# The two-part split of the softmax maxima moves from VectorE to GpSimd in a fused four-layer kernel

## What is computed

```python
scores = jnp.einsum('bhqd,bhkd->bhqk', Q, K) / np.sqrt(HEAD_DIM).astype(np.float32)
attn = jax.nn.softmax(scores, axis=-1)
attn_out = jnp.einsum('bhqk,bhkd->bqhd', attn, V).reshape(B, N, D_MODEL)
```

## Time and profile before

| | |
|---|---|
| median of 3 runs | 379.95 us |
| the profiled execution | 380.56 us, its span 378.6 us |
| TensorE busy | 365.4 us (97%), 3670 matmuls |
| VectorE busy | 327.1 us (86%), 768 instructions |
| ScalarE busy | 316.1 us (83%), 632 |
| GpSimd busy | 187.1 us (49%), 290 |
| most costly group | line 1140 on VectorE, 384 maxima, 240.1 us |
| next | line 966 on ScalarE, 384 exponentials, 201.1 us |

### The profile page before, as it was taken

The page is one execution under the profiler, slowest core; times in us unless marked ns, Lnnn a source line. Parts: engine busy times, 40 slices in busy tenths (PEclk is TensorE's granted clock), DMA queues, the critical chain, the costliest instruction groups (busy, mean ns, idle before and its releaser), DMA issues.

```text
span 378.6 us, 10251 instructions
## 1 busy us (share of the span) xinstructions
PE 365.4 (97%) x3670; PEld 205.8 (54%) x3670; DVE 327.1 (86%) x768; ACT 316.1 (83%) x632; POOL 187.1 (49%) x290
## 2 busy tenths in 40 slices
PE   8689899999999999999999999999999999999997
PEld 3513444556655554555557545465545565457876
DVE  6486999999999989899999899999999999954463
ACT  6302688998999898998999899999889999996674
POOL 5425899866487223794024681225841040115754
PEclk9855999999999999999999999999999999999999
DMA  7810146221004100015000033000050000000001
GB/s 233 227 36 16 56 131 156 93 78 35 0 3 126 47 3 4 2 30 144 2 7 1 2 86 85 4 2 4 3 157 16 3 2 3 2 1 3 3 0 57
DMA packets 17187, 17.63 MB, mean 47 GB/s; under 512 B 2461, under 2 KB 15455, under 8 KB 17121
## 3 DMA queue, kind: packets, MB, share of 16 engines
q1 hardware_dynamic: 15840, 16.19, 15.4%
q10 hardware_dynamic: 1296, 0.79, 0.9%
HBM read 6.62 MB, written 0.52 MB: 19 GB/s over the span
## 4 chain that ended last, share of the span: by engine, by line
PE 66%; DVE 7%; ACT 3%; issue 2%; POOL 0%; ACTq 0%; POOLq 0%
PE pv_ps L841 18%; PE max_ps L651 10%; PE exp_ps L660 10%; PE max_ps L786 8%; PE exp_ps L773 7%; DVE mx L1140 5%; PE exp_ps L621 2%; PE exp_ps L705 2%; PE max_ps L621 2%; PE max_ps L641 2%; ACT probs L966 1%; PE exp_ps L826 1%; PE pv_ps L631 1%; PE max_ps L741 1%; PE exp_ps L641 1%
## 5 line engine op out<-in xcount | busy, mean ns | idle before, releaser
L1140 DVE TENSOR_REDUCE mx<-max_ps 128x1 f32<-128x512 f32 x384 | 240.1, 681 | 10.6 <-PE max_ps L651 9.3
L966 ACT ACTIVATE probs<-exp_ps 128x512 f32<-128x512 f32 x384 | 201.1, 604 | 12.3 <-PE exp_ps L660 11.2
L651 PE MATMUL max_ps<-k_stack,q_stack 64*128 64x512 bf16 x384 | 112.1, 394 | 5.5 <-DMA k_stack<-parts 3.6
L841 PE MATMUL pv_ps<-probs,v_ones 128*32 128x256 f32 x1536 | 103.1, 385 | 0.0
L660 PE MATMUL exp_ps<-q_stack,k_stack 64*128 64x256 bf16 x768 | 99.7, 273 | 0.0
L1160 POOL TENSOR_SCALAR var_eps<-mv 128x2 f32<-128x2 f32 (+2 forms) x33 | 6.4, 195 | 149.1 <-DVE mv L1000 148.7
L841 PEld LDWEIGHTS pv_ps<-probs,v_ones 128*32 128x32 f32 x1536 | 43.4, 109 | 32.3 <-issue 9.0
L651 PEld LDWEIGHTS max_ps<-k_stack,q_stack 64*128 64x128 bf16 x384 | 31.6, 94 | 50.4 <-DVE mx L1140 28.3
L660 PEld LDWEIGHTS exp_ps<-q_stack,k_stack 64*128 64x128 bf16 x768 | 41.7, 95 | 29.0 <-ACT probs L966 12.4
L978 ACT ACTIVATE mrows<-exp_ps 8x256 bf16<-8x256 bf16 x48 | 17.4, 364 | 13.2 <-PE exp_ps L826 13.1
L773 PE MATMUL exp_ps<-hT,w 128*128 128x256 f32 x96 | 26.7, 397 | 0.0
(11 more groups left out here) (128 smaller groups left out, 479.5 us busy)
## 6 DMA issues: line engine op xcount, KB each, us to landing
k_stack<-parts SPq DMA_DIRECT2D x36, 128.0 KB, 2.5
q_stack<-parts SPq DMA_DIRECT2D x30, 128.0 KB
w<-in_w_dram SPq DMA_DIRECT2D x4, 448.0 KB, 3.7
w<-in_w_dram SPq DMA_DIRECT2D x4, 256.0 KB, 3.0
w<-in_ada_dram SPq DMA_DIRECT2D x1, 896.0 KB, 5.4
w<-in_rows_dram SPq DMA_DIRECT2D x1, 832.0 KB, 7.9
q_stack<-mrows SPq DMA_DIRECT2D x48, 4.0 KB
x<-in_x_dram SPq DMA_DIRECT2D x2, 256.0 KB, 3.6
```

Of the source, the lines that this page charges most:

```text
L651: return pe.matmul(max_bank(n), half(q_stack, b, pair, j)[:, t * P:(t + 1) * P], half(k_stack, b, pair, j), start=True, stop=True)
L841: mm = pe.matmul(pv_ps[32 * j:32 * j + 32, cols_of(g // 2)], v_ones[:, b, kt, 4 * g + j, :], probs[:, (4 * i + j) % RING_P, cols_of(of_two ...
L966: act.activation(probs[:, tile % RING_P, :], exp_bank(e), ACT.Exp, scale=SCORE_SCALE[hc // 2 // NB]).then_inc(exp_read, 1)
L1140: dve.tensor_reduce(mx[:, G % 2, t, 2 * (pair % 2) + j:2 * (pair % 2) + j + 1], max_bank(n), AX_X, ALU.max, negate=True).then_inc(max_read, 1)
```

## The change

The two instructions of SPLIT leave VectorE and are issued by GpSimd at the place where SPLIT stands in the same order. The rounding is a scalar multiply by 1 in place of a maximum over one element. GpSimd waits for the last two maxima of the group and for ScalarE's read of ROWS G - 2. VectorE gets one new wait: before the first maximum of group G it waits for split G - 2.

```diff
             for item in ORDER:
                 name, k, h, c = item
-                if name == "SPLIT":
-
-                    G = k
-                    m, pt = mx[:, G % 2].rearrange("p t (a j) -> p t j a", j=HALVES), mparts[:, G % 2]
-                    for j in range(HALVES):
-                        dve.wait_ge(*read_by_dve(("MAX", G // GROUPS, GROUP_BEATS * (G % GROUPS) + GROUP_BEATS - 1, j)))
-                    if G >= 2:
-                        dve.wait_ge(*read_by_act(("ROWS", G - 2, 0, 0)))
-                    settle(dve.tensor_reduce(pt[:, :, 1:3, :], m.unsqueeze(4), AX_X, ALU.max))
-
-                    dve.tensor_tensor(pt[:, :, 0::3, :], m, pt[:, :, 1:3, :], ALU.subtract).then_inc(max_split, 1)
-                elif name == "MAX":
+                if name == "MAX":
...
+                    if G >= 2 and m % GROUP_BEATS == 0:
+                        dve.wait_ge(max_split, G - 1)
...
+            def split_maxima(G):
+
+                m, pt = mx[:, G % 2].rearrange("p t (a j) -> p t j a", j=HALVES), mparts[:, G % 2]
+                for j in range(HALVES):
+                    pool.wait_ge(*read_by_dve(("MAX", G // GROUPS, GROUP_BEATS * (G % GROUPS) + GROUP_BEATS - 1, j)))
+                if G >= 2:
+                    pool.wait_ge(*read_by_act(("ROWS", G - 2, 0, 0)))
+                settle(pool.tensor_scalar(pt[:, :, 1:3, :], m, 1.0, 1.0, ALU.mult, ALU.mult))
+                pool.tensor_tensor(pt[:, :, 0::3, :], m, pt[:, :, 1:3, :], ALU.subtract).then_inc(max_split, 1)
...
             for item in ORDER:
-                dense(item)
+                if item[0] == "SPLIT":
+                    split_maxima(item[1])
+                else:
+                    dense(item)
```

## The result

The changed kernel takes 426.15 us (median of four runs, 424.50 to 426.78) against 379.98 us before on the same chip: a ratio of 1.122, 95% interval 1.118 to 1.126. The profiled execution has a span of 424.0 us.

A forecast was written before the change was run, and what follows sets the result against it. TensorE, in order, was taken to hold the chain of waits (66%), with GpSimd's unbroken runs making splits late. Stalls 40, less 10 drained, less 6 relief, plus 3 clock: +27 us, so 407 us, range 390 to 430.

The forecast's parts named there:

- The rule for late splits: At each ROWS, TensorE stalls until GpSimd's preceding item ends plus 0.5 us for the split; 40 us in all.
- The nine large terms: Stalls at ROWS 2, 6, 8, 9, 12, 13, 21, 29 and 37, 2.9 to 5.8 us each, 36.6 together.
- The small ones: Stalls at splits 20, 28, 35, 45 and the LayerNorm half behind split 26; none above 1.1, 3.4 us together.
- The held-back reductions: On GpSimd, split 5 holds back angle reduction RED 1, making split 6 late, 2.9 us; likewise RED 2 and split 8, 3.5.
- The price of the split on GpSimd: A scalar multiply and a subtraction with a wait between: 0.5 us a split, bounds 0.4 and 1.0.
- What drains during a stall: VectorE and ScalarE drain banks while TensorE stands: up to 1.2 us a stall, 10 us given back, bounds 0 to 13.
- The relief of VectorE: The split leaves VectorE's stream, 17.5 us less; worth 6 us, a third of it.
- The clock: TensorE's granted clock falls once or twice behind the new stalls; 3 us, bounds 0 and 12.
- Rival (a): Stalls right, but little given back or the clock falls several times: +44, 424 us; chance 0.20.
- Rivals (b) to (d): (b) GpSimd's lateness mostly absorbed, 390, chance 0.13; (c) VectorE's maxima set the pace, 373, 0.04; (d) level, near 380, 0.02.
- What I named as signs: Line 826 waits 30 to 45 us, VectorE busy below 80%, GpSimd 15 to 20% of chain, subtraction 0.2 to 0.3 us.

The follow-up runs named there:

- the clock kept up: The changed kernel, with TensorE running 3 to 21 products of zeros ahead of its wait for each of ten late splits; 416.23 us, ratio 1.094.
- the lone one: Only split 37 on GpSimd, the other 47 on VectorE as in the kernel before; 387.22 us, ratio 1.019.
- the placed kernel: Changed kernel with all 48 splits on GpSimd, each inserted in its sequence where its maxima were ready in the kernel before; 382.31 us, ratio 1.005.

## Why the prediction was right, point by point

**The rule for late splits: right.** "The end of the last GpSimd item before it in the order, plus 0.5, against TensorE's start of its ROWS". The nine large terms, forecast and read off the shift from one ROWS to the next: 5.75 and 6.0, 2.9 and 3.4, 3.5 and 2.4, 3.2 and 2.3, 3.3 and 3.3, 3.9 and 4.5, 4.2 and 4.2, 4.0 and 4.3, 5.8 and 5.6. Together 36.6 and 36.0. The small ones came to 2.8 for 3.4: 35 cost 1.2, 45 0.8, 28 0.5, 26 0.3 and 20 nothing. Such a step also holds what the clock cost since the ROWS before, so 8, 9 and 13 differ singly: I read it so that a fall delays the main stream and shortens the next stall, whose end GpSimd's run fixes. With the clock kept up these three are 3.7, 3.3 and 3.9, the nine together 37.8 and the small ones 2.9: 40.7 us of stalls where 40 were forecast.

**The held-back reductions: right**, shown by the kernel with 5 to 8 on GpSimd against the one with 6 and 8.

**The price of the split on GpSimd: right**, 0.49 us for 0.5.

**What drains during a stall: mis-sized.** Forecast 10 us, up to 1.2 a stall. In the kernel with the clock kept up the shift grows by 37.5 us from ROWS 1 to 47, with 40.7 of stalls in it: 3 us came back, and 0.7 and 0.8 of them at ROWS 10 and 23, where the kernel with only 6 and 8 on GpSimd gains nearly as much (0.6 and 0.8) without a stall. The step failed where I took two or three full banks in front of VectorE for granted. VectorE worked for 1.37 us in the stall of ROWS 2, but for 0.48 in that of ROWS 37 and 0.44 in the lone one: there the banks were nearly empty when TensorE stopped.

**The relief of VectorE: mis-sized**, forecast 6 us, net gain measured none. The 17.5 us that I reckoned with are 23.2 by the stream, so the size of what was freed is not what failed. With the late splits on VectorE and 35 on GpSimd 17.7 us are gone from its stream and the ratio is 0.9999; the placed kernel is no faster either. TensorE's weight load still waited for VectorE's maxima 28.0 and 26.1 us in those two (28.3 before), and VectorE's own wait for TensorE rose from 9.3 to 11.8 and 20.7. I had argued from the share of the chain, 7%, and that share told neither that removed work would bring nothing net nor that the same work added would cost in full.

**The clock: mis-sized**, forecast 3 us, measured 9.9. I counted on one or two falls; it fell eight times, at idle times of 2.2 to 5.6 us. The upper bound of 12 held it. I had named a clock under 0.9 after 40 us as the sign that this term would be the larger error; it averaged 0.95, and the error was as large as that of the draining all the same.

So net 40 - 10 - 6 + 3 = 27 was really 41 of stalls, 3 given back, no relief and 10 of clock, which makes 47 or 48 where 46 were measured. The three terms besides the stalls were off by 6 to 7 us each, and all the same way, so the forecast time of 407 was 19 us short and the measurement lies outside my likeliest stretch of 395 to 418. Rival (a), little given back and a clock that falls several times, with 424 and a chance of 0.20, is what happened. The mechanism and the main term were right; that the range of 390 to 430 still held the time is owed to its width. Rivals (b) to (d) fell with the same runs.

**What I named as signs**: the wait at line 826 in about 14 places up to 6 us and of 30 to 45 us in all came (40.5, 15 places). VectorE's busy share fell below 80% (75%). The subtraction on GpSimd took 0.20 us (0.2 to 0.3). GpSimd in the chain of waits with 15 to 20% did not come, since the chain broke off.

Not settled: why the placed kernel is 2 us slower than the kernel before. Its shift rises by 1.3 us at ROWS 7 and by 1.0 at ROWS 39; I did not take this apart. Nor whether a small relief of VectorE is hidden behind these 2 us, and which of TensorE and ScalarE sets the pace once VectorE is relieved.

## What to carry to other kernels

An engine's busy share says nothing about whether it can take a small job on time: with a fixed order, set the end of what stands ahead of the job in its queue against the moment at which the consumer wants it, for each occurrence, and look also at what the job now holds back. Such a sum, 40 us of stalls from the trace of the kernel before, came within 1 us of the stalls read with the clock kept up. That it is also within 2% of the time (420 for 426) is partly luck: it leaves out the clock, 10 us, and what came back, 3. In this kernel, tuned until several engines are nearly level, time added to one cost in full and time removed gave a third or nothing, so measure the worth of relief by taking the work out before moving it.

## What the runs showed of the hardware

In the changed kernel TensorE's granted clock went to its lower level at or behind idle times of 2.2 to 5.6 us, with dense work on both sides, in three cases for some 7 us, and cost between 0.9 and 2.3 us each by the shift at the next ROWS; it did not fall behind idle times of 1.1, 0.7 and 0.6 us there. The length of the last idle time alone did not decide: with the products of zeros it also fell at 90.4 us, behind one of 1.9, and at 42.6, behind one of 0.9, while the kernel before kept it through one of 0.85 at 40 us. Products of zeros during the wait kept it up at most of the stalls and gave 9.9 us back in all. The Trainium skill, "TensorE: Matmul & The Clock Gate", section "What's actually happening", says that the clock is gated by how busy the array has recently been; the trace agrees (0.50 from 51 to 56 us, behind 5.6 us of idling; 0.57 behind the lone stall of split 37, and 1.00 with the products in it).
